# Merged setup phases with three feature blocks ahead, and one compare for a stripe's three codes

## The chip, the cores and the metric

The kernel runs on one core of a Trainium2 chip: TensorE multiplies, VectorE (DVE), ScalarE (ACT) and GpSimd (POOL) work elementwise, and SyncE (SP), ScalarE and GpSimd issue DMAs. The metric is the device time of one launch in microseconds, as the median of several runs.

## The reference

A two-layer graph network on 3750 nodes of 256 features and 63750 edges (sorted by target), of 8 types. Cut to what matters:

```python
h = relu(layernorm(x))
feat_all = einsum('ni,rhid->rnhd', h, conv_weights)          # 8 types, 4 heads of 64
el = sum(feat_all[type, src] * attn_l[type]); er = sum(feat_all[type, dst] * attn_r[type])
alpha = softmax over the edges of each dst of leaky_relu(el + er)
x = x + segment_sum(alpha * feat_all[type, src], dst) + h_bias
h = relu(layernorm(x)) @ W_in + b_in
for l in range(3):
    h = relu(segment_sum(h[src], dst) / deg @ W_agg[l] + h @ W_self[l] + b_hid[l])
x = x + h @ W_out + b_out
```

## The kernel before

The kernel is a row of blocks. At the end of a block all engines meet; `end_phase` (L133) also clears semaphores.

**Setup.** Edge lists are loaded and cast. `tile_ends` (L391) finds the first and last target of each tile of 128 edges while ScalarE and SP load the feature weights. A check block (L432) tests that targets are sorted and sets flags (with sorted edges, flag 0 is off, and all code under it is skipped). `tile_tables` (L624) makes masks, codes and columns of the edges and stores them. The window block (L751) counts, for each of 235 windows (one for 16 target nodes), where its edges begin and end, in a chain of small VectorE operations with some TensorE sums; SP loads x and four vectors in it and stores the row masks `rm_tab` that GpSimd makes. The next block (L900) first sums attention weights into `wlr` (a product on VectorE, one on GpSimd, and two reductions, twice), then takes layer norm over 8 chunks of 4 node blocks: VectorE statistics and scaling, TensorE transposes and products with `wlr`, ScalarE the relu into `hT`. SP issues in it the loads of edge pairs for ten blocks of windows (`EARLY`, `load_pairs` L222: a block's window starts are read into registers, then one DMA for each window), and after them eight stores of `er_tab`.

**The stage that the change feeds.** For each of 30 node blocks (`NBLK`) and each quarter `cc` of a block, the engines walk through one list in the same order: first the windows of the quarter (7 or 8 in a block, so 2, 2, 2 and 1 or 2), then the features of the quarter (512 of the 2048 columns of 128 nodes).

- A window is a stripe of the matrix that counts edges between nodes, 128 x 512. VectorE (`window_dve`) makes three pairs of one-hot matrices: `code` (128 columns, L254) from `rel`, the codes less the window's start, and `other` (512 columns, L255). TensorE (`window_pe`, L265) multiplies them into one of four PSUM banks. ScalarE (`window_act`, L273) evicts the bank to one of four kept windows, and SP (`window_sp`, L279) stores it to `a_tab`. VectorE waits for `built.free`, which begins at `RING`, the number of pairs held, and rises by one with each product.
- A feature quarter is four TensorE instructions (L1336, two matmuls of 512 columns, each in two passes) into one of four other banks, evicted by ScalarE (L1192 and L1194, the second one adding `elr`) into one of two slots, which ScalarE's own queue stores to `feat_tab` (L1198).
- SP at the begin of a block issues the pair loads of block `b + EARLY`, then stores the block's windows as they are evicted; here and there it fills a part of `h_tab` with zeros.

The stage ends when all features are stored: only then GpSimd starts to gather rows of `feat_tab` by edge. The aggregation and the three layers follow; they are not edited.

The wait that the ring's length sets (`DEPTH` is 3, `built.free` begins at `RING`):

```python
dve.wait_ge(built.free, w * DEPTH + DEPTH)
```

Of the kernel before, what the change touches and what calls it, by code (L numbers as in the profile page):

```python
# [66 lines left out]
BLOCK_W = [NREAL * (b + 1) // NBLK - NREAL * b // NBLK for b in range(NBLK)]  # L67
# [3 lines left out]
RING = 8  # L71
# [3 lines left out]
EARLY = 10  # L75
# [24 lines left out]
def gnn_kernel(nc, x, src, dst, etype, conv_w, attn_l, attn_r, h_bias, w_in, b_in, w_agg, w_self,  # L100
               b_hid, w_out, b_out, out):
    ctx = ExitStack()
    with ctx:
        gat = ExitStack()
# [88 lines left out]
        rel = sb("rel", [P, 8, DEPTH])  # L193
# [4 lines left out]
        code = side[:, 0:512].bitcast(F16).rearrange("p (s n) -> p s n", s=RING)  # L198
        other = side[:, 512:2560].bitcast(F16).rearrange("p (s n) -> p s n", s=RING)
# [39 lines left out]
        def shift_codes(dve, b):  # L239

            first, many = FIRST_W[b], BLOCK_W[b]
            dve.wait_ge(s_cl[b % 4], loaded(b))
            dve.wait_ge(built.pair, first * DEPTH + 1)
            dve.tensor_tensor(rel[:, 0:many, :], pairs_in[:, first:first + many, :, 0],
                              win_f[:, first:first + many].unsqueeze(2).to_broadcast([P, many, DEPTH]), ALU.subtract
                              ).then_inc(s_rel, 1)
            dve.wait_ge(s_rel, b + 1)
# [27 lines left out]
        def window_sp(sp, w):  # L275


            sp.wait_ge(built.evicted, w + 1)
            sp.dma_start(a_tab[w * P:(w + 1) * P, :], counts[:, w % KEPT_W, :]).then_inc(s_stored[w % KEPT_W], 16)  # L279

# [28 lines left out]
        s_ld, s_xl, s_at = [nc.alloc_semaphore(a) for a in ("vectors_loaded", "all_x_loaded", "weights_in")]  # L309
        lists_i = stg[:, 5000:5000 + CQ + NTW].bitcast(I32)  # L310
        prod = [stg[:, 4096 + 2048 * i:4096 + 2048 * (i + 1)] for i in range(2)]

        def hrow(i):
            return hT[:, :, :].rearrange("p k n -> p (k n)")[:, i * T:(i + 1) * T].rearrange(
                "p (c j) -> p c j", c=CT)
# [7 lines left out]
        attn = [side[:, 2048 * i:2048 * (i + 1)] for i in range(2)]  # L325

        with nc.Block() as block:
# [31 lines left out]
            def _(dve):  # L359
                for v, buf in zip((N - 1, -1, PADSRC, 0), raw):  # L360
                    dve.memset(buf[:, 3:CR, :], v).then_inc(s_pad, 1)
                dve.memset(ones[:, :], 1.0)
# [24 lines left out]
        def load_attention(eng):  # L387
            for a, buf in zip((attn_l, attn_r), attn):
                eng.dma_start(buf, a.rearrange("(o r) h d -> o (r h d)", o=1).to_broadcast([P, 2048])).then_inc(s_at, 16)

# [78 lines left out]


# [10 lines left out]
        def sort_edges(flag, key_array, other_array):  # L481
# [18 lines left out]
            with nc.Block() as block:  # L500
# [42 lines left out]
                def _(dve):  # L543
                    with when(dve, flag):
                        for v, buf in zip((0, PADSRC, 0), raw_s):
# [77 lines left out]

        def tile_tables(c0, c1, flag=None):  # L624
# [11 lines left out]
            with nc.Block() as block:  # L636
                @block.vector
                def _(dve):
                    with when(dve, flag):
# [19 lines left out]
                        for i, to in enumerate((typ_t, dstloc, fidx_i, code_t, col_t)):  # L659
# [6 lines left out]
                            while at < c1 * P:  # L666
# [15 lines left out]
                                at = end  # L682

# [13 lines left out]
                def _(pool):  # L697
                    with when(pool, flag):
# [9 lines left out]
                        c.link(pool.tensor_copy(dst16[:, 0:nc_, :], cut(dstm)))  # L708

# [15 lines left out]
                def _(act):  # L725
                    with when(act, flag):
# [9 lines left out]
        s_w, s_wc, s_ws, s_ri, s_rw, s_xz = (sem("window_steps"), sem("windows_counted"), sem("window_sums"),  # L736
                                             sem("row_masks"), sem("row_masks_stored"), sem("x_zeroed"))
        begun = stg[:, 1792:1792 + CT * NTW].rearrange("p (c w) -> p c w", c=CT)
        PARTS_T = P // GRAIN
        room = hT[:, :, :].rearrange("p k n -> p (k n)")  # L740
# [6 lines left out]
        cbx = stg[0:1, 7800:7800 + NS * U].rearrange("p (s t) -> p s t", s=NS)  # L747
        cnx = work[0:1, 8192:8192 + NS * U].rearrange("p (s t) -> p s t", s=NS)
        subs_of = lambda a: a[0:1, 0:NS * U].rearrange("p (s t) -> p s t", s=NS)
        DUP = 14  # L750
        with nc.Block() as block:  # L751
            @block.vector
            def _(dve):
                dve.memset(x_all[:, NBLK - 1:32, :], 0.0).then_inc(s_xz, 1)
                c = Chain(dve, s_w)
                starts = win_f[:, 0:NTW].unsqueeze(1).to_broadcast([P, CT, NTW])
                first = small[:, 51:51 + CT]
                c.link(dve.tensor_scalar(ends, key[:, :, GRAIN - 1:P:GRAIN], float(NQ), None, ALU.mult))
                for g in range(PARTS_T):
                    c.link(dve.tensor_tensor(ended[:, g, :, :], ends[:, :, g:g + 1].to_broadcast([P, CT, NTW]), starts,  # L760
                                             ALU.is_lt))
                c.link(dve.tensor_scalar(first, key[:, :, 0], float(NQ), -float(P), ALU.mult, ALU.add))
                c.link(dve.tensor_tensor(begun, first.unsqueeze(2).to_broadcast([P, CT, NTW]), starts, ALU.is_lt))
                c.link(dve.memset(none, 0.0))
                same_t = stg[0:1, 8704:8704 + 512]
# [20 lines left out]
                c.link(dve.tensor_scalar(edge0, PS[0:1, 7, 0:NTW], float(GRAIN), None, ALU.mult))  # L786
                c.link(dve.tensor_scalar(small[0:1, 35:36], small[0:1, 27:28], float(P), None, ALU.mult))
                c.link(dve.tensor_scalar(edge0, edge0, small[0:1, 35:36], None, ALU.min))
                c.link(dve.tensor_tensor(span_w[:, 0:NTW - 1], edge0[:, 1:NTW], edge0[:, 0:NTW - 1], ALU.subtract))
# [1511 lines left out]
```

## Time and profile before

| | us |
|---|---|
| median of 3 runs | 2060.08 |
| lowest and highest | 2058.89, 2077.07 |
| the profiled execution | 2056.71 |
| its span in the trace | 2054.9 |
| TensorE busy | 1770.4 (86%) |
| VectorE busy | 1081.3 (53%) |
| ScalarE busy | 1143.4 (56%) |
| GpSimd busy | 520.6 (25%) |

The span is from the first to the last instruction of one execution, of which all rows below are. Times in rows are microseconds from its start. The busy shares are averages over stages with different limits.

### The profile page before, as it was taken

How to read it: one execution, taken by the hardware profiler on the slowest of the kernel's cores; microseconds unless marked ns; L12 is line 12 of the kernel's file. 1: busy time of each engine (PE TensorE's matmuls, PEld its weight loads, DVE VectorE, ACT ScalarE, POOL GpSimd, SP SyncE). 2: the span in 40 equal slices, each digit the busy share in tenths (PEclk: the TensorE clock that was granted, in tenths of full speed). 3: DMA queues.
4: the chain of work that ended last, by engine and by line, in shares of the span. 5: the costliest groups of instructions: out<-in, count | busy, mean ns of one | idle time of the engine just before them, and what ended most of it. 6: DMA issues, size and time to landing. Idle time of an engine off the chain costs nothing. (4 is left out here: it accounts for less than half of the span.)

```text
span 2054.9 us, 26209 instructions
## 1 busy us (share of the span) xinstructions
PE 1770.4 (86%) x7604; PEld 1230.3 (60%) x7605; DVE 1081.3 (53%) x3126; ACT 1143.4 (56%) x2498; POOL 520.6 (25%) x544
## 2 busy tenths in 40 slices
PE   2169999999488789798797946999989999999998
PEld 1064344444366556565575624777777777877777
DVE  6858788888266676766767535545450000301011
ACT  0035455555387779797797724444444545644442
POOL 3400000000577777777777300000000000000000
PEclk9669999999697889798898888999999999999999
DMA  6215555656655566565665316332333333363432
GB/s 164 50 14 180 172 192 181 200 189 210 187 155 154 153 181 177 151 197 153 182 177 152 109 56 192 109 121 92 111 93 116 115 115 116 96 209 124 133 123 57
DMA packets 285221, 290.67 MB, mean 141 GB/s; under 512 B 88673, under 2 KB 248102, under 8 KB 284806
## 3 DMA queue, kind: packets, MB, share of 16 engines
q1 hardware_dynamic: 239318, 187.28, 29.9%
q0 software_dynamic: 23952, 66.46, 12.0%
q10 hardware_dynamic: 21792, 35.10, 4.7%
q8 instruction: 64, 1.05, 0.2%
q14 instruction: 95, 0.78, 0.1%
HBM read 201.26 MB, written 87.48 MB: 141 GB/s over the span
## 5 line engine op out<-in xcount | busy, mean ns | idle before, releaser
L1152 POOL DMA_INDIRECT work<-feat_tab,fidx_i x499 | 477.0, 956 | 583.5 <-issue 581.4
L2128 PE MATMUL PS<-a_pe,y_hi 128*128 128x512 f32 (+2 forms) x1440 | 555.8, 392 | 33.1 <-ACT a_pe L2025 33.1
L2128 PE MATMUL PS<-a_pe,y_lo 128*128 128x512 f32 (+2 forms) x1440 | 535.7, 378 | 0.0
L2025 ACT ACTIVATE a_pe<-a_in 128x1536 fp32r<-128x1536 f16 (+1 forms) x240 | 329.6, 1377 | 341.7 <-PE PS L2128 328.5
L2128 PEld LDWEIGHTS PS<-a_pe,y_hi 128*128 128x128 f32 (+1 forms) x1440 | 273.4, 190 | 102.6 <-ACT a_pe L2025 34.8
L1221 ACT ACTIVATE work<-work 128x64 f32<-128x64 f32 x1344 | 325.2, 332 | 0.0
L2128 PEld LDWEIGHTS PS<-a_pe,y_lo 128*128 128x128 f32 (+1 forms) x1440 | 273.7, 190 | 55.0 <-issue 6.7
L1396 PE MATMUL PS<-work,stg 128*128 128x260 f32 x1008 | 288.3, 435 | 8.0 <-ACT work L1221 6.2
L255 DVE TENSOR_SCALAR side<-iota_c,work 128x512 f16<-128x512 f16 x705 | 245.8, 349 | 0.0
L1396 PEld LDWEIGHTS PS<-work,stg 128*128 128x128 f32 x1008 | 205.6, 215 | 65.7 <-issue 16.0
L1336 PE MATMUL PS<-wbuf,hT 128*128 128x512 f32 x480 | 226.1, 593 | 0.0
L2232 DVE TENSOR_TENSOR mean<-PS,rdeg 128x1024 f32<-128x1024 f32 (+1 forms) x24 | 27.2, 1135 | 363.3 <-PE PS L2128 363.0
L273 ACT ACTIVATE side<-PS 128x512 f16<-128x512 f32 x235 | 128.4, 595 | 144.2 <-PE PS L265 69.5
L254 DVE TENSOR_SCALAR side<-iota_c,rel 128x128 f16<-128x128 f16 x705 | 177.0, 251 | 48.9 <-PE PS L265 48.2
L265 PE MATMUL PS<-side 128*128 128x512 f16 x705 | 173.6, 381 | 23.3 <-DVE side L255 14.4
L265 PEld LDWEIGHTS PS<-side 128*128 128x128 f16 x705 | 68.2, 98 | 149.7 <-DVE side L255 36.5
L1346 PE MATMUL PS<-er_win,stg 128*128 128x32 f32 x1008 | 133.2, 292 | 24.5 <-ACT stg L1207 24.5
L1346 PEld LDWEIGHTS PS<-er_win,stg 128*128 128x128 f32 x1008 | 128.2, 208 | 28.3 <-ACT stg L1207 26.5
L1336 PEld LDWEIGHTS PS<-wbuf,hT 128*128 128x128 f32 x480 | 91.6, 191 | 74.9 <-issue 57.7
L1192 ACT ACTIVATE stg<-PS 128x512 f32<-128x512 f32 x120 | 71.9, 599 | 39.6 <-PE PS L1336 37.7
L1599 DVE TENSOR_TENSOR work<-work,PS 128x1024 f32<-128x1024 f32 x42 | 51.3, 1221 | 70.5 <-ACT work L1213 69.1
L1590 DVE TENSOR_TENSOR stg<-PS,dstloc 128x512 f32<-128x512 f32 x126 | 86.4, 687 | 1.5
(257 smaller groups left out, 1669.1 us busy)
## 6 DMA issues: line engine op xcount, KB each, us to landing
a_in<-a_tab SPq DMA_DIRECT2D x210, 384.0 KB, 3.2
feat_tab<-stg ACTq DMA_DIRECT2D x120, 260.0 KB, 2.1
a_tab<-side SPq DMA_DIRECT2D x235, 128.0 KB, 1.8
stg<-dst_tab SPq DMA_DIRECT2D x42, 384.0 KB
work<-feat_tab,fidx_i POOLq DMA_INDIRECT x499, 3.0
h_tab<-outs SPq DMA_DIRECT2D x42, 130.0 KB, 2.7
h_tab<-outs SPq DMA_DIRECT2D x8, 520.0 KB, 4.2
stg<-h_tab SPq DMA_DIRECT2D x8, 520.0 KB, 4.1
```

Source lines behind the costliest of these rows:

```text
L254: dve.tensor_scalar(code[:, s, :], iota_c[:, 0:P], rel[:, k, j:j + 1], None, ALU.is_equal)
L255: dve.tensor_scalar(other[:, s, :], iota_c[:, :], pairs_in[:, w, j, 1:2], None, ALU.is_equal).then_inc(built.pair, 1)
L265: pe.matmul(PS[:, BBS[w % len(BBS)], :], code[:, s, :], other[:, s, :], start=(j == 0), stop=(j == DEPTH - 1)).then_inc(built.free, 1)
L273: act.activation(counts[:, w % KEPT_W, :], PS[:, BBS[w % len(BBS)], :], ACT.Copy).then_inc(built.evicted, 1)
L1152: pool.indirect_dma_start(out=ring[:, s, 0:FE], out_offset=None, in_=feat_tab[:, :], in_offset=bass.IndirectOffsetOnAxis(ap=idx, axis=0)). ...
L1221: ins = act.activation(a, a, ACT.Copy, scale=ring[:, s, F + h:F + h + 1])
L1336: mm = pe.matmul(PS[:, cc, :], hT[:, k, b * P:(b + 1) * P], wc[:, k, cc * 512:(cc + 1) * 512], start=(k == 0), stop=(k == K2 - 1))
L1346: mm = pe.matmul(PS[:, ERB, u * RH:(u + 1) * RH], onehotT[:, u * P:(u + 1) * P], er_win[:, :], start=True, stop=True)
L1396: mm = pe.matmul(PS[:, OUTS[j], 0:EXT], onehot[:, t, :], ring[:, j * U + t, 0:EXT], start=(t == 0), stop=(t == U - 1), skip_group_check=True)
L1590: dve.tensor_tensor(onehot[:, q * QT:(q + 1) * QT, :], IOTA_PS.unsqueeze(1).to_broadcast([P, QT, P]), dstloc[:, tiles_of(i, j, q, QT)].uns ...
L2025: act.activation(a_pe[:, load % A_PE, :, 0:n], a_in[:, load % A_IN, :, 0:n], ACT.Copy).then_inc(s_conv, 1)
L2128: mm = pe.matmul(SUMS(ug, n)[:, f, :], y[0:rows_of, kb, f * P:(f + 1) * P], a_pe[0:rows_of, load % A_PE, kb % KB, 0:n], start=(kb == 0 and ...
```

## The change

- The check block now also loads x and the four vectors on SP (`load_nodes`); the last rows of x are zeroed in the first block.
- The attention sums move to the end of the unconditional `tile_tables` block (`attention_sums`, `attention_products`), behind its VectorE and GpSimd work.
- The window block and the layer norm block are one. VectorE finds the edges' starts (`edge0`, `edge_i`) first and tells SP (`s_wd`), then does layer norm, then the rest of the counting. TensorE does the sum for the starts, layer norm, features of four quarters, two sums for the counting, features of eight more quarters. ScalarE evicts these twelve after layer norm. SP waits for x and for the starts, then issues pair loads, `er_tab` stores and row masks.
- `AHEAD = 3` blocks of features are so done in setup; the stage walks over 27 blocks, and its 235 windows are spread over these (8 or 9 in a block; with 9 the first quarter has three). `EARLY` is 8 instead of 10.
- `code` of a window is made by one compare of 3 x 128 with two tensor operands instead of three of 128 with a scalar operand each. The ring has 6 pairs instead of 8 (4 instead of 8 in a branch that isn't taken here).
- Buffers move: the edge rows leave `hT` for a tensor of their own, which is freed after the block, `elr` has a tensor of its own, and scratch places shift.

```diff
-BLOCK_W = [NREAL * (b + 1) // NBLK - NREAL * b // NBLK for b in range(NBLK)]
+AHEAD = 3
+BLOCK_W = [0] * AHEAD + [NREAL * (b + 1) // (NBLK - AHEAD) - NREAL * b // (NBLK - AHEAD) for b in range(NBLK - AHEAD)]
-RING = 8
+RING, RING_AGAIN = 6, 4
-EARLY = 10
+EARLY = 8
...
         def window_dve(dve, w, k):
             dve.wait_ge(built.free, w * DEPTH + DEPTH)
+            at = w * DEPTH % RING
+            dve.tensor_tensor(code[:, at:at + DEPTH, :], iota_c[:, 0:P].unsqueeze(1).to_broadcast([P, DEPTH, P]),
+                              rel[:, k, :].unsqueeze(2).to_broadcast([P, DEPTH, P]), ALU.is_equal)
             for j in range(DEPTH):
                 s = (w * DEPTH + j) % RING
-                dve.tensor_scalar(code[:, s, :], iota_c[:, 0:P], rel[:, k, j:j + 1], None, ALU.is_equal)
                 dve.tensor_scalar(other[:, s, :], iota_c[:, :], pairs_in[:, w, j, 1:2], None, ALU.is_equal
                                   ).then_inc(built.pair, 1)
...
+        def sum_features(pe, q):
+            b, cc = divmod(q, 4)
+            if q >= 4:
+                pe.wait_ge(s_fe, 2 * (q - 3))
+            for k in range(K2):
+                mm = pe.matmul(PS[:, cc, :], hT[:, k, b * P:(b + 1) * P], wc[:, k, cc * 512:(cc + 1) * 512],
+                               start=(k == 0), stop=(k == K2 - 1))
+            mm.then_inc(s_fm, 1)
+
+        def keep_features(act, q):
+            b, cc, slot = q // 4, q % 4, q % 2
+            act.wait_ge(s_fm, q + 1)
+            if q >= 2:
+                act.wait_ge(s_fs[slot], 16 * (q // 2))
+            act.activation(fout[:, slot, :, 0:F], PS[:, cc, :].rearrange("p (r f) -> p r f", r=2), ACT.Copy
+                           ).then_inc(s_fe, 1)
...
+            act.dma_start(feat_tab[0:PADSRC * R, :].rearrange("(n r) f -> n r f", r=R)[
+                b * P:(b + 1) * P, 2 * cc:2 * cc + 2, :], fout[:, slot, :, :]).then_inc(s_fs[slot], 16)
...
+        def load_all_x(sp, turn=1):
+            sp.wait_ge(s_xz, turn)
+            sp.dma_start(x_all[:, 0:FULL, :], x[0:FULL * P, :].rearrange("(b p) f -> p b f", p=P)).then_inc(s_xl, 16)
+            sp.dma_start(x_all[0:N - FULL * P, FULL, :], x[FULL * P:N, :]).then_inc(s_xl, 16)
...
+        def attention_sums(dve):
+            dve.wait_ge(s_at, 16 * (K2 * R + 2))
+            for i in range(2):
+                dve.tensor_tensor(prod[0], wc[:, 0, :], attn[i], ALU.mult).then_inc(s_pr, 1)
+                dve.wait_ge(s_pr, 3 * i + 1)
+                for k in range(K2):
+                    if k == 1:
+                        dve.wait_ge(s_pp, i + 1)
+                    dve.tensor_reduce(wlr[:, k, i * RH:(i + 1) * RH], prod[k].rearrange("p (c d) -> p c d", d=D), AX.X,
+                                      ALU.add).then_inc(s_pr, 1)
+                    dve.wait_ge(s_pr, 3 * i + k + 2)
...
+                c.link(dve.tensor_copy(edge_i[:, :], edge0))
+                dve.sem_inc(s_wd, 1)
+                dve.wait_ge(s_xr, 1)
+                ln_stats(dve, x_rows(0), 0, 0, s_bs, s_vr)
+                over_chunks(dve, step)
+                keep(NC - 2, 0)
+                keep(NC - 1, 1)
...
+                act.wait_ge(s_ee, NC)
+                for q in range(4 * AHEAD):
+                    keep_features(act, q)
...
                 over_chunks(pe, step)
                 halves(NC - 1, (NC - 1) % 2)
+                pe.wait_ge(s_ht, 2 * NC)
+                for cc in range(4):
+                    sum_features(pe, cc)
+                pe.wait_ge(s_ee, NC)
+                for c in range(CT):
+                    pe.matmul(PS[0:1, 5, 0:NTW], one_c, ended[:, PARTS_T - 1, c, :], start=(c == 0), stop=(c == CT - 1))
+                pe.wait_ge(s_w, PARTS_T + 7)
...
+                mm.then_inc(s_wc, 1)
+                for q in range(4, 4 * AHEAD):
+                    sum_features(pe, q)
...
-                for b in range(EARLY):
+                sp.wait_ge(s_wd, 1)
+                for b in range(AHEAD, AHEAD + EARLY):
                     load_pairs(sp, b)
                 over_chunks(sp, store)
+                sp.wait_ge(s_ri, 12)
+                at = 0
+                for a, n in ((csx, U + 1), (cbx, U), (cnx, U)):
+                    for h in range(H):
+                        sp.dma_start(rm_tab[:, at:at + n].unsqueeze(0), a).then_inc(s_rw, 16)
```

## Rows read from the trace of the kernel before

**Rows 1.** Timeline: first code and last feature products of the stage; start, length, engine, line.

```profile
148.73 0.26 DVE L254 TENSOR_SCALAR side<-iota_c,rel 128x128 f16<-128x128 f16 x1
...
518.18 1.88 PE L1336 MATMUL PS<-wbuf,hT 128*128 128x512 f32 x4
```

**Rows 2.** Stretches: window, length, busy PE, PEld, DVE, ACT, POOL, clock, DMA.

```profile
170.00:190.00 20.00, 20.00 (x67) 8.85 (x66) 17.92 (x82) 10.80 (x25) 0.00 (x0) 1.00 0.64 214
```

**Rows 3.** Timeline of the stage, one quarter of a block.

```profile
183.69 1.46 PE L265 MATMUL PS<-side 128*128 128x512 f16 x6
...
184.99 1.88 PE L1336 MATMUL PS<-wbuf,hT 128*128 128x512 f32 x4
...
186.71 1.46 PE L265 MATMUL PS<-side 128*128 128x512 f16 x6
...
187.13 0.26 DVE L254 TENSOR_SCALAR side<-iota_c,rel 128x128 f16<-128x128 f16 x1 [0.30 <-PE PS L265]
187.29 0.35 DVE L255 TENSOR_SCALAR side<-iota_c,work 128x512 f16<-128x512 f16 x1
...
187.56 0.25 DVE L254 TENSOR_SCALAR side<-iota_c,rel 128x128 f16<-128x128 f16 x1
```

**Rows 4.** Waits in the stage (149 to 521): total, times, longest.

```profile
ACT side L273 <- DMA a_tab<-side: 62.0, 19, 6.2
DVE side L254 <- PE PS L265: 48.2, 109, 2.9
...
PE PS L265 <- ACT side L273: 8.8, 7, 2.4
```

**Rows 5.** Timeline of SP's issues: pair loads in the first and the twentieth block.

```profile
151.00 4.03 SPq L228 DMA_DIRECT2D work<-pair_tab  x8
...
392.75 4.72 SPq L228 DMA_DIRECT2D work<-pair_tab  x8
```

**Rows 6.** Timeline of VectorE in setup; idle time before in brackets.

```profile
17.22 0.69 DVE L435 TENSOR_TENSOR stg<-hT 128x508 f32<-128x508 f32 x1 [0.64 <-PEq L394]
...
28.44 0.69 DVE L641 SCALAR_TENSOR_TENSOR hT<-hT 128x512 f32<-128x512 f32 x1 [4.68 <-PEq L394]
...
44.20 0.70 DVE L754 MEMSET work<- 128x768 f32 x1 [2.10 <-PEq L636]
...
54.10 1.39 DVE L762 TENSOR_SCALAR small<-hT 128x7 f32<-128x7 f32 x1
...
74.91 6.63 DVE L925 TENSOR_TENSOR stg<-wbuf,side 128x2048 f32<-128x2048 f32 x1 [2.83 <-PEq L751]
...
86.21 2.29 DVE L925 TENSOR_TENSOR stg<-wbuf,side 128x2048 f32<-128x2048 f32 x1
...
95.30 1.40 DVE L881 BATCH_NORM_STATS2 stats<-work 128x6 f32<-128x256 f32 x4
...
135.03 0.42 DVE L908 TENSOR_SCALAR stg<-PS 128x256 f32<-128x256 f32 x1 [1.36 <-PE PS L972]
```

**Rows 7.** Timeline of SP's issues and of TensorE's counting in setup.

```profile
45.36 6.41 SPq L857 DMA_DIRECT2D work<-in_x  x1
...
53.91 0.52 SPq L862 DMA_DIRECT2D bh_c<-in_L_gnn_b_hid  x1
...
57.49 3.00 PE L829 MATMUL PS<-stg,ones 128*1 128x240 f32 x14 [0.41 <-DVE stg L763]
...
65.08 5.40 SPq L868 DMA_DIRECT2D rm_tab<-stg  x8
...
76.44 24.64 SPq L228 DMA_DIRECT2D work<-pair_tab  x33
...
135.59 5.62 SPq L999 DMA_DIRECT2D er_tab<-stg  x8
```

**Rows 8.** Timeline: a two-operand operation of 384 columns.

```profile
700.27 0.56 DVE L1515 TENSOR_TENSOR tsel<-PS,tmask 128x384 f32<-128x384 f32 x1
```

**Rows 9.** A stretch of layer norm: window, length, TensorE busy, clock, DMA.

```profile
120.00:128.00 8.00, 8.00 (x40) 0.50 0.12 7
```

More of the change, by code:

```diff
@@ L361, in _ @@
                     dve.memset(buf[:, 3:CR, :], v).then_inc(s_pad, 1)
+                dve.memset(x_all[:, FULL:32, :], 0.0).then_inc(s_xz, 1)
                 dve.memset(ones[:, :], 1.0)
@@ L468, in _ @@
                 load_attention(act)
+            @block.sync
+            def _(sp):
+                load_nodes(sp)
         SW = -(-(E + ADDED * N) // (4 * P)) * 4
@@ L622, in gnn_kernel, with attention_products @@
         dst16 = stg[:, 8000:8000 + CR * P // 2].bitcast(I16).rearrange("p (c j) -> p c j", c=CR)
+        def attention_sums(dve):
[9 more added lines that the diff above has]
+                    dve.wait_ge(s_pr, 3 * i + k + 2)
+        def attention_products(pool):
+            pool.wait_ge(s_at, 16 * (K2 * R + 2))
+            for i in range(2):
+                if i == 1:
+                    pool.wait_ge(s_pr, 3)
+                pool.tensor_tensor(prod[1], wc[:, 1, :], attn[i], ALU.mult).then_inc(s_pp, 1)
         def tile_tables(c0, c1, flag=None):
@@ L753, in _, with x_rows, keep, step @@
             def _(dve):
-                dve.memset(x_all[:, NBLK - 1:32, :], 0.0).then_inc(s_xz, 1)
+                def x_rows(c):
+                    return lambda b: x_all[:, bass.ds(c * 4 + b, 1), :].rearrange("p o f -> p (o f)")
+                def keep(c, slot):
+                    dve.wait_ge(s_el, c + 1)
+                    dve.tensor_scalar(elr[:, bass.ds(c * 4, 4), :, :],
+                                      PS[:, 4 + slot, 0:256].rearrange("p (b i n) -> p b i n", b=4, i=2),
+                                      0.0, None, ALU.add).then_inc(s_ee, 1)
+                def step(c, slot, first, last):
+                    if not last:
+                        ln_stats(dve, x_rows(c + 1), c + 1, 1 - slot, s_bs, s_vr)
+                    if not first:
+                        wait_past(dve, s_tp, c - 1)
+                    ln_finish(dve, x_rows(c), c, slot, s_sd, s_rs, s_hn, hN[:, slot, :, :])
+                    if not isinstance(c, int) or c > 1:
+                        keep(c - 2, slot)
+                with when(dve, 0):
+                    dve.memset(x_all[:, FULL:32, :], 0.0).then_inc(s_xz, 1)
                 c = Chain(dve, s_w)
@@ L802, in _ @@
                 spots = TURNS_SORTED
-                row = stg[0:1, 8704:8704 + spots]
-                below = stg[0:1, 8768:8768 + (NC - 1) * spots].rearrange("p (c j) -> p c j", c=NC - 1)
+                row = stg[0:1, 4480:4480 + spots]
+                below = stg[0:1, 4544:4544 + (NC - 1) * spots].rearrange("p (c j) -> p c j", c=NC - 1)
                 c.link(dve.tensor_copy(row, base_i[0:1, 0:spots * G:G]))
@@ L816, in _ @@
                 c.link(dve.tensor_copy(cuts_i[0:1, NC:NC + 1], turns_i[0:1, 0:1]))
-            @block.tensor
-            def _(pe):
-                for g in range(PARTS_T):
-                    pe.wait_ge(s_w, g + 2)
-                    for c in range(CT):
-                        pe.matmul(PS[0:1, 7, 0:NTW], one_c, ended[:, g, c, :], start=(g == 0 and c == 0),
-                                  stop=(g == PARTS_T - 1 and c == CT - 1))
-                for c in range(CT):
-                    pe.matmul(PS[0:1, 5, 0:NTW], one_c, ended[:, PARTS_T - 1, c, :], start=(c == 0), stop=(c == CT - 1))
-                pe.wait_ge(s_w, PARTS_T + 3)
-                for c in range(CT):
-                    mm = pe.matmul(PS[0:1, 6, 0:NTW], ones[:, 0:1], begun[:, c, :], start=(c == 0),
-                                   stop=(c == CT - 1))
-                mm.then_inc(s_wc, 1)
             @block.gpsimd
@@ L994, in _ @@
                 sp.wait_ge(s_ld, 16 * 4)
+                sp.wait_ge(s_xl, 32)
+                with when(sp, 0):
+                    load_all_x(sp, 2)
+                    sp.wait_ge(s_xl, 64)
+                sp.sem_inc(s_xr, 1)
                 def store(c, slot, first, last):
@@ L1495, in _ @@
                 w = 0
-                for b in range(NBLK):
+                for b in range(AHEAD, NBLK):
                     many = BLOCK_W[b]
@@ L1681, in _ @@
                 w = 0
-                for b in range(NBLK):
+                for b in range(AHEAD, NBLK):
                     if b + EARLY < NBLK:
@@ L1848, in _ @@
                     dve.sem_inc(s_rt, 1)
-                    dve.sem_inc(again.free, RING)
+                    dve.sem_inc(again.free, RING_AGAIN)
                     dve.sem_inc(again.evicted, 1)
```

211 lines of the change are left out of this document (83 added, 128 removed).

## The prediction

> **What bounds the kernel now.** I read the timeline first, in order of time, since the change touches only the first quarter of the span. The setup phases reach 148.73 us, where VectorE makes the first window codes; the last feature product ends at 518.18 + 1.88 = 520.06 [rows 1]. The rest, gathering and then the layers, waits for all feature rows and is not edited. So two lengths matter: 148.73 of setup and 371.3 of the stage that builds the count matrix beside the features.
>
> In the stage TensorE is busy 20.00 of 20.00 us at a granted clock of 1.00, which is 2.4 GHz [rows 2]. The steady pattern: six window products start at 183.69, four feature products at 184.99, the next six at 186.71 [rows 3]. A quarter of a feature block with two windows thus takes 3.02 us (3.01 over many), 0.215 for each window product and 0.43 for each feature product. VectorE needs 0.16 for a code and 0.27 for the other one-hot before the next begins, 0.43 a pair and 1.28 a window [rows 3]: 2.57 for two windows, and it then waits for TensorE (48.2 us over the stage) [rows 4]. TensorE binds, VectorE has 15% to spare. 115 quarters of 3.01 and 5 with one window (2.37) give 358.0; the other 13.3 are start and stalls. 8.8 of them are TensorE waiting for ScalarE's evictions, and ScalarE's longest sum of waits there is for window stores to land, 62.0 us in 19 waits [rows 4]. That is SP: a block's pair loads (0.50 each) stand in front of its window stores. SP needs 12.72 us a block ((392.75 - 151.00) / 19) while it has pair loads [rows 5], where TensorE's own work is 11.9. SP is the second bound.
>
> In setup VectorE is the chain: check until 23.76 (28.44 less 4.68 idle), tables until 42.10, counting until 72.08, attention sums until 95.3, layer norm until 135.45; then SP issues eight stores until 141.21, and 7.5 us later the first window starts [rows 1, 6, 7].
>
> **The merged compare.** Three scalar compares of 128 columns cost 3 x 0.16 = 0.48. The new one has two tensor operands, 384 columns, one of them f32; the nearest row is the tensor_tensor of 384 columns at 0.56 [rows 8], and operations overlap by 0.08 (0.35 long, next one after 0.27 [rows 3]), so 0.48. A window stays at 1.28 (with three others of 0.27). Bounds: 0.26 if it ran at the rate of the others per column, 0.56 with no overlap. I take 0.48, since the row has the same size and a f32 operand. Nothing is gained, and TensorE hides VectorE anyway.
> The Trainium skill, VectorE: DVE Perf Modes, in its rules for kernel authors, says to minimize the number of operations, and puts a fixed 151 cycles on each. By that alone the merge would save two fixed costs, an estimate of 0.31 us a window, and the stall worked out below would halve, for 2046 instead of 2052. Its table of modes speaks against that: a two-operand compare with f32 has only the slowest mode where the scalar form with f16 has the fastest. No row shows the merged form with an f16 and a f32 source at this size.
>
> **The ring of two whole windows.** Before, with eight pairs, window w could be coded after the first product of window w-2; now only after its third. The first product releases VectorE 0.42 after the group starts (186.71 to 187.13 [rows 3]), the third 0.85 after. With two windows a quarter, VectorE is done at 0.85 + 2.56 = 3.41, and the last pair is wanted at 3.01 + 1.07: hidden, 0.6 to spare, less 0.3 at a block's shift of codes. But 235 windows over 27 blocks make 19 blocks of nine, so 19 quarters have three windows. The third one starts its codes at 0.85, has its first pair at 0.85 + 0.48 + 0.35 = 1.68, is multiplied from about 1.82 (0.15 for semaphore and weights), its last product starts 0.54 later and ends the group at 2.57; TensorE alone would be there at 1.94. Short by 0.63, 19 times: 12.0 us. Bounds: 0 and 0.85 each. The next quarter has caught up again.
>
> **Features ahead.** 12 quarters x 4 x 0.43 = 20.6 us of TensorE work leave the stage. New stage: 108 x 3.01 = 325.1, plus 19 x (0.64 + 0.63) = 24.1, together 349.2. To that the 13.3 of start and stalls. On SP a block of nine has one load and one store more; 12.72 and 0.87 windows more of 1.2 each (a load of 0.50, a store of 0.70 [rows 5, 7]) give some 13.8 a block against TensorE's 12.9: the same closeness, a longer hold (6.5 instead of 6.0). I add 2, bounds -5 and +22 (a rival). Stage: 364.5, 6.8 shorter.
>
> **Setup, step by step.**
> - Check block. SP now issues the load of x and four vectors there. Before, the second part of x was held for 6.41 behind the first, and the last vector was issued at 54.43 [rows 7]; with 0.4 for the first part that is 9.5 us, and from 17.22 [rows 6] gives 26.7, later than VectorE's 23.76. So the block ends 2.95 later. Bounds 0 (the issue no longer held back) and 7 (attention's loads share the queues).
> - Tables: shifted to 31.4 to 45.05. Their stores run beside x's arrival; the attention sums behind hide a delay up to 16 us, after that it is full price.
> - Attention sums move behind the tables. GpSimd's first product is now done beforehand, so the first half costs three operations of 2.29, 6.9 instead of 11.3; the second half, where GpSimd's product is waited for, stays 9.05 (86.21 to 95.30) [rows 6]. 16.0, bounds 13.7 (six times 2.29) and 20.35. Ends 61.0; join 2.1, as before the counting (the idle at 44.20 [rows 6]): 63.1. What is gone is the 2.83 join at 74.91.
> - Ends of edges: 9.9 less the 0.7 memset, 1.6 for the last sums on TensorE, 1.3 for four small operations (my estimates; the full-precision counting product takes 3.0 for 14 [rows 7]): edges are known at 75.2. x has been there for long.
> - Layer norm: 40.15 (95.30 to 135.45) as before, to 115.4. GpSimd's row masks run beside its first part; 0 to 2, I take 0.
> - Behind it, VectorE has 18.0 (54.10 to 72.08) less 1.2 for what went ahead (my estimate, 0.3 each), plus some 1.5 of waiting for TensorE's sums: 133.7. TensorE: four features 6.9, counting 1.5 + 3.0 [rows 7], eight features 13.8, ScalarE's last eviction and issue 1.1: 115.4 + 26.3 = 141.7. Each feature's eviction waits for the store two before; ScalarE needs some 1.6 a quarter for that, under 1.72.
> - SP has the pair loads first: 78 took 59.15 for ten blocks (76.44 to 135.59 [rows 7]), which is 0.50 each and 2.0 a block. Now 69 in eight blocks: 50.5, to 125.7. Behind them, which is new, er stores 5.6 and twelve row-mask stores at 0.675, 8.1 [rows 7]: 139.4. They are queued behind the wait for the edges; nothing but the end of the phase waits for them.
> SP and ScalarE end within 1 us of each other. From SP's issue 7.5 to the first window gives 146.9; from ScalarE's end 5.5 (2 of the 7.5 are taken as SP's landing) gives 147.2. So setup ends 1.5 earlier, with three blocks of features done. Joined: 1.5 + 6.8 = 8.3 us. The profiled execution took 2056.7 (span 2054.9), 3.4 under the median 2060.1, so 2048.4 for such an execution and **2052** for the median.
>
> **Rivals.**
> - A, faster: the third window of a quarter isn't short, because TensorE is stalled by SP then anyway or the codes come faster, and the check block isn't held. 12.0 + 3 more: 2037. For it: the stalls of SP and of the ring need not add. Against: the wait of VectorE for TensorE is in every cycle of the trace [rows 3, 4], and the ring only makes it longer.
> - B, slower: SP takes over the stage. It decides once SP needs more than TensorE's 12.9 a block. If nine loads, nine stores and the register loads before them take 14.1, the 19 blocks cost 22 us more: 2074. For: SP is already at 12.72 and its holds already cost 8.8. Against: in 255 us of such blocks TensorE was stalled for no more than 8.8, in 7 waits [rows 4], so most holds are absorbed by the four banks and four kept windows.
> - C, no gain: TensorE gets the lower level (1.2 GHz) for the features in setup. In layer norm 8 us had 0.50 although TensorE was busy throughout [rows 9], and each feature then takes 3.4: up to 20.6 more on the chain that ends the phase, 2072; with one half of them, 2062. Against: it would be busy without a gap from layer norm on, and such a stretch is at 1.00 [rows 2].
>
> **How the numbers follow.** The measurement tells 1% (20.6 us), no less. Forecast 0.55, A 0.22, B 0.11, C 0.12. Below 2039.5 lie most of A and a little of the forecast: 0.22. Above 2080.7 lie only B or C beyond their price, or both at once: 0.09. The forecast's own bounds (attention -2 to +4, check block -3 to +4, stall -12 to +4, SP -5 to +5) make 2038 to 2062. Taking in A's time and half of B and C gives 2034 to 2069.
>
> **What would show it.** First window code at 147 and last feature product near 512; the merged compare 0.56 long; VectorE's wait for L265 longer, and TensorE waiting for VectorE some 0.6 in one quarter of a block, 19 times; attention sums 16 us; SP and ScalarE last in the merged phase. Wrong: a setup over 155 (C, or x's issue), SP over 13.5 a block (B), or no short quarter (A).

## The result, and the profile after

The changed kernel took 2088.81 us (median of 4, 2079.65 to 2098.86) against 2062.34 for the kernel before on the same chip: ratio 1.0122, 95% interval [1.0093, 1.0151]. It is 1.2% slower; 2052 was forecast, with a range to 2069. The profiled execution took 2088.69, with a span of 2086.6.

First the timeline of the changed kernel at the two ends of the stage (start, length, engine, line, operation):

```profile
161.25 0.56 DVE L256 TENSOR_TENSOR side<-iota_c,rel 128x384 f16<-128x384 f16 x1
...
539.63 1.88 PE L291 MATMUL PS<-wbuf,hT 128*128 128x512 f32 x4
```

They answer to [rows 1]. The first window code comes at 161.25 (148.73 before, 147.2 forecast), and the last feature product ends at 541.51 (520.06 before). So setup is 12.5 longer and the stage, 380.3, is 8.9 longer, though 12 of its 120 feature quarters went. These 21.5 us are two thirds of the 31.7 between the two spans. The last 10.2 lie behind the stage, in code that isn't edited; more on them below.

**Setup.** The timeline of SP, VectorE and GpSimd, which answers to [rows 6, 7]; idle time before an instruction stands in brackets:

```profile
17.68 14.46 SPq L364 DMA_DIRECT2D work<-in_x  x1
...
34.23 0.52 SPq L437 DMA_DIRECT2D bh_c<-in_L_gnn_b_hid  x1
```

```profile
39.34 0.69 DVE L714 SCALAR_TENSOR_TENSOR index_rows<-index_rows 128x512 f32<-128x512 f32 x1 [15.48 <-PEq L443]
...
47.25 4.60 DVE L722 TENSOR_SCALAR index_rows<-index_rows 128x512 f32<-128x512 f32 x1
...
57.20 2.29 DVE L681 TENSOR_TENSOR stg<-wbuf,side 128x2048 f32<-128x2048 f32 x1
...
70.93 2.29 DVE L686 TENSOR_REDUCE wlr<-stg 128x32 f32<-128x2048 f32 x1 [2.14 <-POOL stg L695]
75.83 0.74 DVE L880 TENSOR_SCALAR index_rows<-index_rows 128x28 f32<-128x28 f32 x1 [2.62 <-PEq L709]
...
87.99 1.41 DVE L835 BATCH_NORM_STATS2 stats<-work 128x6 f32<-128x256 f32 x4
...
129.09 0.42 DVE L861 TENSOR_SCALAR elr<-PS 128x256 f32<-128x256 f32 x1 [1.36 <-PE PS L996]
```

```profile
46.75 4.82 POOL L695 TENSOR_TENSOR stg<-wbuf,side 128x2048 f32<-128x2048 f32 x1
64.22 6.61 POOL L695 TENSOR_TENSOR stg<-wbuf,side 128x2048 f32<-128x2048 f32 x1 [12.65 <-DVE wlr L686]
```

The operation of L722 as the kernel before has it (its L649):

```profile
36.35 0.43 DVE L649 TENSOR_SCALAR hT<-hT 128x512 f32<-128x512 f32 x1
```

The reader is to see two things. The second part of x's load keeps SP for 14.46 us (6.41 in [rows 7]), and since all engines meet at the end of the block, VectorE is idle for 15.48 before the tables. And L722 takes 4.60 us where the same operation took 0.43 before the change: it runs from 47.25 to 51.85 beside GpSimd's product of 46.75 to 51.57. The other steps took about what was forecast: attention sums 57.20 to 73.22, 16.0 as forecast; layer norm from 87.99 to 129.51.

**The stage.** Stretches (window, length, busy us of PE, PEld, DVE, ACT and POOL with counts, clock, DMA share, GB/s), which answer to [rows 2]:

```profile
200.00:240.00 40.00, 36.38 (x122) 15.39 (x121) 32.60 (x103) 21.28 (x50) 0.00 (x0) 1.00 0.55 181
240.00:280.00 40.00, 35.38 (x113) 15.00 (x112) 30.65 (x96) 19.30 (x46) 0.00 (x0) 0.96 0.49 157
...
360.00:400.00 40.00, 34.03 (x106) 14.25 (x106) 28.82 (x91) 19.96 (x46) 0.00 (x0) 0.91 0.52 168
...
440.00:480.00 40.00, 39.28 (x132) 17.35 (x131) 35.80 (x113) 24.20 (x55) 0.00 (x0) 1.00 0.59 203
```

TensorE is idle for 3.6 to 6.0 us of 40 in the first three, while SP has pair loads to issue, and for 0.72 in the last, where it has none left. The waits of 161 to 541, which answer to [rows 4] (total, times, longest):

```profile
ACT side L278 <- DMA a_tab<-side: 75.0, 16, 8.5
...
DVE side L256 <- PE PS L270: 64.3, 114, 4.6
...
PE PS L270 <- ACT side L278: 23.3, 19, 4.6
PE PS L270 <- DVE side L260: 13.0, 13, 8.7
```

TensorE's wait for evictions grew from 8.8 in 7 waits to 23.3 in 19. One of them in the timeline, in the block that begins at 369.95:

```profile
369.95 5.64 SPq L231 DMA_DIRECT2D work<-pair_tab  x9
...
375.63 7.09 SPq L284 DMA_DIRECT2D a_tab<-side  x9
377.54 0.60 ACT L278 ACTIVATE side<-PS 128x512 f16<-128x512 f32 x1 [8.48 <-DMA a_tab<-side]
...
378.19 1.46 PE L270 MATMUL PS<-side 128*128 128x512 f16 x3 [4.59 <-ACT side L278]
...
379.44 3.47 PE L291 MATMUL PS<-wbuf,hT 128*128 128x512 f32 x4
```

SP issues nine pair loads. The first window store comes behind them at 375.63; ScalarE, which had waited 8.48 us for a kept slot, evicts at 377.54, and TensorE, which had no bank for 4.59 us, goes on at 378.19. Then it runs slower for a while: the four feature products take 3.47 in place of 1.88 and three window products 1.46 in place of 0.81. There the granted clock is at the lower level, 1.2 GHz, which makes the stretch's mean 0.91; TensorE had been idle for 4.59 us before.

### The profile page after: what moved, and what is told of

Its sections match the earlier page's. It is cut to its first block and busy times, and to the rows that moved or that the text cites. A ratio compares the mean times of both kernels' runs of the same rounds, so it can differ in the third digit from the quotient of the medians.

```text
span 2086.6 us, 25723 instructions
## 1 busy us (share of the span) xinstructions
PE 1791.2 (86%) x7604; PEld 1238.2 (59%) x7605; DVE 1075.4 (52%) x2653; ACT 1144.8 (55%) x2498; POOL 518.5 (25%) x544
## 3 DMA queue, kind: packets, MB, share of 16 engines
q0 software_dynamic: 23952, 66.46, 12.1%
## 5 line engine op out<-in xcount | busy, mean ns | idle before, releaser
L291 PE MATMUL PS<-wbuf,hT 128*128 128x512 f32 x480 | 230.4, 607 | 0.0
L270 PE MATMUL PS<-side 128*128 128x512 f16 x705 | 177.2, 383 | 36.4 <-ACT side L278 23.3
L260 DVE TENSOR_SCALAR side<-iota_c,work 128x512 f16<-128x512 f16 x705 | 204.7, 346 | 0.0
L256 DVE TENSOR_TENSOR side<-iota_c,rel 128x384 f16<-128x384 f16 x235 | 130.2, 554 | 64.4 <-PE PS L270 64.3
```

What stands on the lines that cost most here:

```text
L256: dve.tensor_tensor(code[:, at:at + DEPTH, :], iota_c[:, 0:P].unsqueeze(1).to_broadcast([P, DEPTH, P]), rel[:, k, :].unsqueeze(2).to_broad ...
L260: dve.tensor_scalar(other[:, s, :], iota_c[:, :], pairs_in[:, w, j, 1:2], None, ALU.is_equal).then_inc(built.pair, 1)
L270: pe.matmul(PS[:, BBS[w % len(BBS)], :], code[:, s, :], other[:, s, :], start=(j == 0), stop=(j == DEPTH - 1)).then_inc(built.free, 1)
L291: mm = pe.matmul(PS[:, cc, :], hT[:, k, b * P:(b + 1) * P], wc[:, k, cc * 512:(cc + 1) * 512], start=(k == 0), stop=(k == K2 - 1))
```

## The experiments

Stage is the time from the first window product to the start of the last feature product: 149.4 to 519.5 before, 162.2 to 540.9 after. The runs named c, d and f were made on three other chips, one for each letter, where gathering takes about 815 us in every kernel in place of 630 and the kernel before 2248 to 2252. Runs g were made on a fourth, where gathering takes about 630 and the kernel before 2064.8. So only ratios, setup and stage are compared across chips, and each ratio is to the kernel before on the same chip. After and f2 are one kernel, and their stages are 2.3 us apart.

| run | first window | stage | ratio, 95% |
|---|---|---|---|
| before | 149.4 | 370.1 | 1 |
| after | 162.2 | 378.7 | 1.0122 [1.0093, 1.0151] |
| f2 changed kernel again | 161.6 | 376.4 | 1.0096 [1.0073, 1.0119] |
| c1 ring 8, three compares | 160.9 | 376.7 | 1.0065 [1.0042, 1.0088] |
| c2 before with compare and ring 6 | 150.4 | 369.7 | 0.9989 [0.9974, 1.0004] |
| c3 x loaded late | 153.3 | 374.7 | 1.0038 [1.0019, 1.0057] |
| f3 attention loaded later | 156.5 | 377.1 | 1.0090 [1.0071, 1.0109] |
| c4 pairs on GpSimd | 162.4 | 349.3 | 0.9964 [0.9950, 0.9977] |
| d3 c4 and ring 8 | 161.9 | 342.5 | 0.9923 [0.9895, 0.9952] |
| d1 c4 and x in the tables block | 151.3 | 349.7 | 0.9915 [0.9889, 0.9942] |
| f1 all three | 151.7 | 341.2 | 0.9897 [0.9880, 0.9913] |
| d2 before, pairs on GpSimd | 149.6 | 359.2 | 0.9955 [0.9936, 0.9974] |
| d4 one block ahead | 151.5 | 376.5 | 1.0030 [1.0010, 1.0050] |
| f4 loads between stores | 162.1 | 349.8 | 0.9951 [0.9931, 0.9971] |
| g2 six kept windows | 161.7 | 350.0 | 0.9977 [0.9958, 0.9996] |
| g3 before, loads between stores | 149.9 | 359.1 | 0.9950 [0.9931, 0.9970] |
| g1 f4, x in tables, ring 8 | 151.0 | 343.0 | 0.9870 [0.9833, 0.9907] |

**Does the loss repeat, and is it in setup and stage?** f2 is the changed kernel as it is.

> The changed kernel as it is, beside the experiments on their chip. If the loss comes from the setup phases and the build stage alone, it repeats here with the first window at 162 us, the stage at 376 to 380 us and a ratio of 1.009 to 1.012, though the gather phase is longer on this chip. If a part of the loss came from the phases behind the stage, the ratio differs from 1.012 while setup and stage repeat.

Setup and stage repeat: f2's last feature product ends at 538.59, 18.5 us behind the 520.06 of the kernel before, and 2269.9 against 2247.96 is 21.9. So setup and stage carry most of the loss. The first comparison's extra 10.2 are 6.6 in gathering and 3.6 behind it. Gathering (first to last gather) took 627.8 us before and 634.4 after, but 637.9 in g3, whose gathering comes from the kernel before, 631.3 in g1 and 629.0 in g2. From the last gather to the end it is 902.5 before and 906.1 after, and 905.0, 909.6 and 906.5 in g3, g2 and g1. Both vary by more than these differences whatever the kernel, and no cause in the change was found.

**The compare and the ring.** c1 undoes both in the changed kernel, c2 puts both into the kernel before.

```diff
-RING, RING_AGAIN = 6, 4
+RING, RING_AGAIN = 8, 4
...
-            dve.tensor_tensor(code[:, at:at + DEPTH, :], iota_c[:, 0:P].unsqueeze(1).to_broadcast([P, DEPTH, P]),
-                              rel[:, k, :].unsqueeze(2).to_broadcast([P, DEPTH, P]), ALU.is_equal)
...
+                dve.tensor_scalar(code[:, s, :], iota_c[:, 0:P], rel[:, k, j:j + 1], None, ALU.is_equal)
```

> The changed kernel with the ring of eight pairs and the three scalar compares back; all else as changed. Stage is from the first window code to the last feature product: 371.3 us before, 380.3 after. Theory SP: what stalls TensorE in the stage is SP's queue (a block of nine windows has its nine pair loads in front of its stores, and only eight windows fit into the four banks and four kept slots), so the stage stays at 374 to 381 and TensorE's waits for ScalarE stay above 15 us. Theory ring: the short quarters with three windows cost 0.63 each, so the stage falls by 12, to 368.

> The kernel before with one part alone: one compare for three codes and the ring of six pairs. No quarter has three windows here and a block has seven or eight. Both theories: the compare lasts 0.55, VectorE needs 1.27 a window instead of 1.28, the stage stays within 3 us of 371. If the ring alone hurts even with two windows a quarter, the stage is longer by 5 or more.

c1's stage stays at 376.7, with TensorE still waiting 25.8 us for evictions. Its ratio lies 0.3% under f2's, which was measured on another chip; the two intervals overlap, and setup and stage show 0.4 us of it. c2 changes nothing, 0.9989, in a kernel whose quarters have two windows at most. So this part neither wins nor loses in the stage while SP holds it back.

**The pair loads off SP.** c4 lets GpSimd issue the stage's pair loads (with registers and semaphores of its own, not shown); d2 does it in the kernel before; d3 adds the ring of eight and the three compares to c4.

```diff
+                for b in range(AHEAD + EARLY, NBLK):
+                    wait_past(pool, s_rel, b - EARLY - AHEAD)
+                    load_pairs(pool, b)
...
-                    if b + EARLY < NBLK:
-                        load_pairs(sp, b + EARLY)
```

> The changed kernel with the pair loads of the stage (19 blocks) issued by GpSimd, which has nothing else to do there, instead of SP. Theory SP: SP's holds are gone, TensorE's wait for ScalarE falls from 23 us to under 5, the granted clock stays at 1.00 in all of the stage, and the stage falls from 380 to 355 to 360. Theory ring: the stage falls by no more than 5.

> The kernel before with the pair loads of its stage (20 blocks) issued by GpSimd instead of SP, nothing else. Theory SP: SP was the second bound before the change too, so its 8.8 us of stalls go and the stage falls from 370 to 360 (358 of TensorE's own work and the start). If SP matters only with nine windows in a block (more than the eight places), the stage stays within 3 us of 370.

> The changed kernel with the stage's pair loads on GpSimd and the ring of eight pairs with three compares. With SP out of the way the ring's own price shows: by the waits of TensorE for VectorE in the run with pairs on GpSimd (6.8 us in 19 waits besides the first) the stage falls from 349 to 342; by the prediction's 0.63 for each of 19 it falls to 337; if VectorE's time for compares counts, it does not fall.

Some 27 us of the stage go, more than the 20 to 25 expected, and the kernel is faster than the one before. The waits of c4 that TensorE has left are those of the ring (161 to 500; the stage ends at 512):

```profile
PE PS L277 <- DVE side L267: 16.7, 19, 10.3
```

10.3 is the start; the other 18 take 6.4, 0.36 each, and a nineteenth comes behind 500. Stretches of d3, where these are gone too (TensorE's busy time is the third number):

```profile
200.00:240.00 40.00, 40.00 (x135) 17.65 (x133) 37.74 (x170) 23.37 (x54) 14.92 (x26) 1.00 0.59 190
```

The ring costs 6.8 us (349.3 to 342.5) once nothing hides it. d3 undoes the compare too, but VectorE's time for a window is the same in both forms by the traces: 0.47 for the merged compare and 3 x 0.16 for the three. And the kernel before had the same loss in a smaller size: 370.1 falls to 359.2.

**Fewer windows in a block.** d4 sets `AHEAD = 1`, so that 26 of 29 blocks have eight windows.

> The changed kernel with one block of features ahead instead of three: 29 blocks, of which 3 have nine windows and 26 have eight; pair loads on SP. Theory eight places: the stalls come from blocks with nine windows, so although TensorE has 13.8 us more work in the stage, it is no longer than with three ahead: 364 to 370 (379 with the change). Theory of load: SP is short in every block, and the stage is 380 or more.

Neither theory fits. TensorE's own work there is 116 quarters of 3.01 and 3 third windows of 0.64, 351.1, and the stage is 25 longer; in the changed kernel (337.2) it is 41 longer, in the one before (358.0) 12. So fewer windows in a block take off a part, and blocks of eight in eight places still have holds: TensorE waits 15.3 us for evictions, and SP's period, from one block's first pair load to the next, is 13.6. Why d4 is worse than the kernel before stays open. Five blocks of that one have seven windows, where SP can catch up; d4 has none of these and three of nine. No run tried that alone.

**Sum of SP's work, its order, or the places?** f4 deals the loads out, one behind each store, with the same instructions on the same engine; g3 does it in the kernel before; g2 keeps SP's order but has six kept windows. The first piece of code is f4's (`each_pair` is `load_pairs` as a generator, one load at a time), the second g2's.

```diff
...
-                    if b + EARLY < NBLK:
-                        load_pairs(sp, b + EARLY)
+                    pairs = each_pair(sp, b + EARLY) if b + EARLY < NBLK else iter(())
                     for _ in range(BLOCK_W[b]):
                         window_sp(sp, w)
+                        next(pairs, None)
                         w += 1
+                    for _ in pairs:
+                        pass
```

```diff
-KEPT_W = 4
+KEPT_W = 6
...
-        counts = side[:, 2560:3584]
+        counts = side[:, 2048:3584]
```

> The changed kernel with SP's pair loads of the stage dealt out, one behind each window store, in place of all eight or nine ahead of the block's stores. Theory that SP's total issue work is the bound: the stage stays at 370 to 380 us and the ratio at 1.008 to 1.012. Rival, that the row of loads holds back the stores of its block and only four windows are kept: the evictions never wait long, the stage falls to 350 to 362 us, ratio 0.999 to 1.004.

> The changed kernel with six kept windows in place of four, in the room that the ring of six freed; SP's order stays as it is. If windows stop because a block's nine don't fit into four PSUM banks and four kept slots while SP issues the row of loads, ten places hold them: the waits of ScalarE for stores shrink to a few us, SP's nine stores go out in one row of about 6.2 us, and the stage falls to 352 to 364 us (SP's row of loads and gap, 7.4 us, and 6.2 us, are 13.6 us a block), ratio 0.998 to 1.004. If the number of places is not what counts, the stage stays at 374 to 380 us, ratio 1.008 to 1.012.

> The kernel before with its pair loads dealt out between the stores. Taking the loads off SP had shortened its stage from 370 to 359 us. If order is the limit there too, this does the same: 358 to 362 us and a ratio of 0.993 to 0.997. If in the kernel before, with eight windows a block at most and eight places, it is SP's total work beside TensorE's that counts, the stage stays at 366 to 370 us and the ratio at 0.998 to 1.001.

This settles it: 349.8 and 350.0, at or just under the short end of what was expected (350 and 352) and the same as with the loads on GpSimd. The ratios, 0.9951 and 0.9977, are below what was expected too. SP's sum of work was not the bound. g2's own timeline of SP shows how:

```profile
386.40 5.70 SPq L231 DMA_DIRECT2D work<-pair_tab  x9
392.14 5.01 SPq L284 DMA_DIRECT2D a_tab<-side  x9
400.13 4.48 SPq L231 DMA_DIRECT2D work<-pair_tab  x9
```

The row of loads is as long as before the edit (5.64, 5.70), but the nine stores behind it take 5.01 in place of 7.09: with four slots SP waits in the middle of them for stores to land and evictions to follow. SP's period of a block falls from 14.7 to 13.2, counted over all 19 blocks with loads as the prediction counted its 12.72. g3's 359.1 says that the same order already cost the kernel before its 11 us.

**x's load.** c3 issues it in the merged block, d1 in the block of the tables behind their stores; f3 leaves it in place and moves ScalarE's attention loads one block later. The place that f3's loads leave:

```diff
             @block.scalar
             def _(act):
-                load_attention(act)
```

> The changed kernel with the load of x and the four vectors moved out of the check block to the start of the merged block on SP. Theory issue: in the check block SP was held 14.5 us behind x's first part, which kept all engines at the end of the block; without it the tables start at about 28.4 instead of 39.3, and the second window code comes at 150 to 152 instead of 161. Rival: x is then late for layer norm (13 us of transfer against 12 us of edge counting), and the pair loads behind it on SP are 9 us later, so that SP ends the phase and half of the 11 us comes back: 155.

> The changed kernel with the stage's pair loads on GpSimd, and x and the four vectors loaded on SP in the tables block, behind the three table stores, where nothing but the attention sums follows. Stage as in the run with pairs on GpSimd, 349 us, by both theories. Theory issue: the check block ends as before the change, x is there before layer norm, and the first window code comes at 149 to 151 (161 with the change, 152 with x loaded late). Rival: x's rows then travel beside the attention sums and slow them or the stores, 155. Ratio to before by the first 0.990, by the second 0.993.

> The changed kernel with ScalarE's two attention loads moved from the block that issues x's load to the next block, where ScalarE issues them ahead of its copies; x's load stays where it is. Theory: SP's second x load is held for 14.5 us because the attention vectors, spread over 128 rows, are fetched at the same time; then it falls to 6 or 7 us, the tile tables start at about 31 us in place of 39, and the first window comes at 153 to 155 us, ratio 1.004 to 1.007. Rival: the hold is x's own descriptors behind the weights loaded just before; then it stays at 14 us, and first window and ratio stay at 162 us and 1.009 to 1.012.

Lines of c3, d1 and f3, the second part of x each time:

```profile
65.96 6.08 SPq L364 DMA_DIRECT2D work<-in_x  x1
```

```profile
43.74 7.43 SPq L371 DMA_DIRECT2D work<-in_x  x1
```

```profile
17.68 9.80 SPq L364 DMA_DIRECT2D work<-in_x  x1
```

Away from the start the issue takes 6 to 7 us, and beside the tables nothing waits for it: the first window comes 11 us earlier (151.3 against 162.4 in c4). c3, with x in the merged block, gets back less of it (153.3), its first code coming at 152.31, nearer to the issue theory than to the rival's 155. f3 came out between its theories: without the attention loads beside it the hold is 9.80, so they are 4.4 of the 8.1 too much. What holds the other 3.7 wasn't isolated; the feature weights' loads, issued just before, are the candidate. The 5 us that f3 wins in setup are 0.2% and cannot be told in its ratio, which is within the interval of f2's.

**Together.**

> Three edits at once on the changed kernel: the stage's pair loads on GpSimd, x loaded in the block of the tile tables, and the ring of eight stripes with three compares. If their gains are independent, the first window comes at 151 us and the stage, from the first window product to the last feature product's start, takes 342.5 us; against 162 and 379 us in the changed kernel that is 48 us less, and a ratio to the kernel before of 0.987 to 0.990. If they overlap, as they would if GpSimd's loads or the ScalarE evictions became the bound, the stage stays above 346 us and the ratio is that of the run without the larger ring, 0.9915.

> Loads dealt out between the stores, x loaded in the block of the tile tables, ring of eight stripes with three compares; no work moves to GpSimd. If the order of SP's queue is all that its stage needs, this equals the run with GpSimd's loads and the same two other edits: first window 151 to 152 us, stage 341 to 344 us, ratio 0.988 to 0.992. If SP's sum of work (about 13.3 us of issue and waits a block) becomes the bound once the ring no longer slows TensorE, the stage stays at 348 to 352 us and the ratio at 0.991 to 0.995.

The gains add up, and GpSimd isn't needed: g1, with x loaded in the tables block, the loads between the stores and the ring of eight, takes 2036.62 against 2064.8, ratio 0.987. Its interval overlaps that of f1, so which of the two is best is not shown. A stretch of g1:

```profile
200.00:240.00 40.00, 40.00 (x136) 17.55 (x135) 36.67 (x169) 24.04 (x54) 0.00 (x0) 1.00 0.61 195
```

Its stage of 343.0 is 5.8 above the sum of TensorE's own work (108 quarters of 3.01 and 19 third windows of 0.64, 337.2).

## Why the prediction was wrong

The sum was 14.1 too small in setup (161.25 for 147.2) and 15.8 in the stage (380.3 for 364.5). Two of the prediction's own signs of being wrong came: a setup over 155, by x's issue, and SP over 13.5 a block.

- **Check block: failed.** The step took the hold of x's issue, 6.41, from a place where nothing else was loading. It was 14.46 and the tables started at 39.34 for 31.4, 7.9 later. The value taken was 2.95 of delay, and it was 10.9. The upper bound named one cause that f3 bears out (attention's loads, 4.4 of it), but its 7 was too small as well.
- **Tables: failed by 4.2.** They were taken as shifted unchanged. But the attention products moved with the sums, and GpSimd's first one ran beside L722, 4.60 for 0.43, which is all of the 4.2. "GpSimd's first product is now done beforehand" was costed as a gain of 4.4 without asking what it runs beside. The loss had only moved: before, VectorE's product beside the same GpSimd product took 6.63 for 2.29 [rows 6]. Attention sums themselves: 16.0, right.
- **Join and edges:** the join is 2.6 against 2.1, and 75.83 to 87.99 is 12.2 against 12.1. **Layer norm** 41.5 against 40.15, for which no cause was looked for. **Tail:** ScalarE's last issue ends at 155.2, 25.7 behind layer norm for 26.3 forecast, and SP's last about 3 before it. These held.
- **Merged compare: right.** It is 0.554 long, and the next operation begins 0.48 later (161.25 to 161.73), the value taken. By the Trainium skill's rule to minimize the number of operations (VectorE: DVE Perf Modes, Rules for kernel authors) it should have been shorter. The trace disagrees here: three scalar compares of 0.16 cost the same 0.48.
- **Ring: right mechanism, mis-sized term.** 0.63 for each of 19 quarters was forecast, 12.0; with nothing in front of it the trace shows 0.36, and the stage 6.8. The price of the whole quarter with three windows was near all the same: 4.28 forecast (3.01 + 0.64 + 0.63), and 4.19 in f4, from the feature products at 470.94 to those at 475.13. That is in part luck, since with the ring of eight such a quarter takes 3.79 (d3, 464.65 to 468.44) and not 3.65. In the changed kernel itself the ring shows only in part (TensorE's wait for VectorE is 13.0, less 8.7 at the start is 4.3), and c1's stage won nothing by taking it away: rival A's reason, that stalls of SP and of the ring don't add, was right, while its time was not.
- **Stage, SP's term: failed, and here rival B was the case.** "To that the 13.3 of start and stalls" carried over a sum of which 8.8 had been read as SP's holds, and d2 and g3 show that 11 of it were. The "2" added for SP was then 18: the holds cost 28.9 in the changed kernel (378.7 against 349.8) and 10.9 before. B's price, 22 us at 14.1 a block, was near; SP needed 14.7. But B's reason, issue work above TensorE's, is not what the runs showed: the same work in another order is enough. The 8.8 itself, "stalled for no more than 8.8, in 7 waits", was read rightly: over 160 to 520 TensorE's busy time falls short by 8.9 in all, and taking the holds away gave 10.9. What failed was to take from it that "most holds are absorbed by the four banks and four kept windows" in the changed kernel too. The holds come in clusters, which the one stretch that the prediction showed, 20 us at 20.00, doesn't touch. The kernel before, at 200 to 240, the same view:

```profile
200.00:240.00 40.00, 36.47 (x119) 15.76 (x119) 32.03 (x147) 20.02 (x48) 0.00 (x0) 1.00 0.52 170
```

TensorE lost 3.5 of 40 us there. A block of nine windows has a ninth load in the row and one window more than the eight places hold, and TensorE's waits for evictions went from 8.8 to 23.3. That places are short is shown by g2; that the ninth window is all of it is not, since d4 with eight in most blocks waits 15.3.

- **The clock,** rival C: not in setup, where features ran at 0.43 a product (14.00 us for 32). It came in the stage instead, behind the stalls, with three stretches of 40 us at 0.96, 0.96 and 0.91: some 6.8 us of TensorE work at the full level (3.2 in f2, with two stretches at 0.96). No term had it there. It is within the 28.9, since f4 has 1.00 in these stretches.

In sum: 13.5 of setup's 14.1 are x's hold (7.9), the tables (4.2) and layer norm (1.4). The stage's 15.8 are SP's holds with the clock behind them, 28.9 where the forecast had 10.9 and 2. Its other terms, 351.6, meet the 351.4 of f4 (161.11 to 512.51), though not each by itself: the ring was overpriced, and the third window and the stage's start were underpriced.

## What to carry to other kernels

When an engine's queue mixes two kinds of DMAs, count not its sum but its longest row of the one kind, against the buffers that the other kind drains: two more kept windows, or loads dealt out between the stores, were worth 27 us here. Before carrying "start and stalls" into a forecast, ask which queue makes the stalls and what the change does to its longest row: 8.8 us of waits, read rightly, became 23.3 and some lower clock. A load that is moved early meets other loads, and an operation that is moved beside another engine's is priced with that neighbour.

## What had not been expected of the hardware

- One DMA instruction of SP keeps its queue for 14.2 to 14.7 us at one place and 6.0 to 7.4 at others, for the same transfer of x; the attention loads beside it make 4.4 of that.
- A VectorE operation on 512 columns took 4.60 in place of 0.43 beside GpSimd's product of 2048, in every run that moved the product there, while a product and a reduce of VectorE ran at their usual 2.29 beside the second one, which itself took 6.61 for 4.82. In the four such pairs of the two kernels the one that started first kept its time. GpSimd's began at 46.75 and at 74.89 (before), and VectorE's behind it, at 47.25 and 74.91, took 4.60 and 6.63. VectorE's began at 64.17 and at 86.21 (before), and GpSimd's behind it, at 64.22 and 86.26, took 6.61 both times. This is read from the rows; no edit moved one of a pair alone.
- In an otherwise busy stage TensorE's granted clock fell to the lower level for a few us behind some stalls and not behind others as long. In the changed kernel it fell behind idle times of 2.21 (twice) and 4.59 us, and not behind one of 2.84; in d4 it fell behind one of 2.32.
- Between SP's last store and its first pair load lie 1.2 to 1.8 us in some blocks and 2.5 to 3.1 in others, where no fill of `h_tab` stands between them,, in nearly the same pattern in after, c1, f2 and g2; the cause is open, and nothing above rests on it.
